# Row maxima from the high parts of q and k, with two 64-row matmuls in place of two 128-row ones

## What is computed

```
q, k, v = split_heads(x @ Wq.T), split_heads(x @ Wk.T), split_heads(x @ Wv.T)     # B=4, H=16, N=1024, d=64
s = (q @ k.T) / 8
m = max(s, axis=-1)
p = exp(s - m)
out = (p / (sum(p, axis=-1) + 1e-10)) @ v          # then @ Wo.T + bo, residual, feed-forward
```

## Time and profile before

| | |
|---|---|
| median of three runs | 1754.97 us |
| the profiled execution: its time | 1758.2 us |
| its span | 1756.4 us |
| PE (matmul) busy | 1617.6 us, 92% |
| DVE busy | 1431.2 us, 81% |
| POOL busy | 1252.1 us, 71% |
| ACT busy | 1070.3 us, 61% |
| mean granted TensorE clock | 0.977 |

### The profile page before, as it was taken

The page is one execution under the profiler, slowest core; times in us unless marked ns, Lnnn a source line. Parts: engine busy times, 40 slices in busy tenths (PEclk is TensorE's granted clock), DMA queues, the critical chain, the costliest instruction groups (busy, mean ns, idle before and its releaser), DMA issues.

```text
span 1756.4 us, 35369 instructions
## 1 busy us (share of the span) xinstructions
PE 1617.6 (92%) x13825; PEld 1192.2 (68%) x13825; DVE 1431.2 (81%) x2463; ACT 1070.3 (61%) x2222; POOL 1252.1 (71%) x1369
## 2 busy tenths in 40 slices
PE   4899999999999999999999999999999999999966
PEld 2576677777776667776667776667767676777754
DVE  7777776666788888888888888988888888888777
ACT  3466566666666656666666666665666665666533
POOL 3577777777777777777777777777777777777853
PEclk8899999999999999999999999999999999999987
DMA  5110001111111001111001111000111100111000
GB/s 133 25 25 14 19 20 26 26 25 26 26 26 27 15 15 27 27 26 27 15 16 26 27 27 25 21 20 15 27 27 26 27 15 15 27 27 26 3 4 12
DMA packets 26373, 43.24 MB, mean 25 GB/s; under 512 B 3744, under 2 KB 18016, under 8 KB 26208
## 3 DMA queue, kind: packets, MB, share of 16 engines
q1 hardware_dynamic: 26208, 40.99, 10.6%
HBM read 4.80 MB, written 2.10 MB: 4 GB/s over the span
## 4 chain that ended last, share of the span: by engine, by line
PE 52%; DVE 41%; ACT 3%; issue 2%; POOL 1%; DMA 0%; DVEq 0%; ACTq 0%; POOLq 0%
PE ob L534 14%; DVE negm L767 12%; PE sm L488 10%; PE st L506 7%; PE st L508 7%; PE mb L433 4%; DVE k_l L718 3%; DVE q_hl L718 2%; DVE xn L934 2%; PE mb L449 2%; DVE qv L919 2%; DVE q_small L915 2%; DVE qw L926 2%; PE mb L444 2%; DVE qw L924 2%
## 5 line engine op out<-in xcount | busy, mean ns | idle before, releaser
L381 POOL TENSOR_TENSOR p_low<-probs 128x512 f16<-128x512 f32 x1024 | 1086.0, 1070 | 424.5 <-ACT probs L616 422.6
L616 ACT ACTIVATE probs<-st 128x512 f32<-128x512 f32 x1024 | 607.9, 597 | 423.9 <-PE st L508 421.6
L767 DVE TENSOR_REDUCE negm<-sm 128x1 f32<-128x1024 f32 x512 | 624.6, 1220 | 150.8 <-PE sm L488 147.5
L506 PE MATMUL st<-q_hl,k_hh 128*128 128x512 f32 x1024 | 465.7, 455 | 0.0
L488 PE MATMUL sm<-k_hh,q_hl 128*128 128x512 f32 x1024 | 370.4, 443 | 65.1 <-DVE negm L767 62.4
L508 PE MATMUL st<-q_hm,k_l 66*128 66x512 f32 x1024 | 409.5, 400 | 0.0
L534 PEld LDWEIGHTS ob<-v,probs 128*128 128x128 bf16 x4096 | 236.5, 98 | 141.7 <-issue 141.7
L534 PEld LDWEIGHTS ob<-v,p_low 128*128 128x128 f16 x4096 | 234.8, 97 | 144.0 <-issue 130.2
L534 PE MATMUL ob<-v,probs 128*128 128x129 f16 x4096 | 325.1, 222 | 0.0
L534 PE MATMUL ob<-v,p_low 128*128 128x129 f16 x4096 | 323.0, 221 | 1.8 <-POOL p_low L381 1.8
L506 PEld LDWEIGHTS st<-q_hl,k_hh 128*128 128x128 f32 x1024 | 194.8, 190 | 40.6 <-issue 0.9
(11 more groups left out here) (145 smaller groups left out, 1611.2 us busy)
## 6 DMA issues: line engine op xcount, KB each, us to landing
k_hh<-k_hh SPq DMA_DIRECT2D x64, 256.0 KB, 3.3
q_hm<-q_hl SPq DMA_DIRECT2D x64, 256.0 KB, 3.4
x<-x SPq DMA_DIRECT2D x4, 512.0 KB, 7.2
q_hm<-m_high SPq DMA_DIRECT2D x128, 2.0 KB
q_hm<-m_low SPq DMA_DIRECT2D x128, 2.0 KB
out<-x SPq DMA_DIRECT2D x24, 64.0 KB, 1.5
probs<-wq SPq DMA_DIRECT2D x1, 512.0 KB, 5.6
probs<-wk SPq DMA_DIRECT2D x1, 512.0 KB, 6.8
```

Source lines behind the costliest of these rows:

```text
L381: return pool.tensor_tensor(p_low[b][:, j, :], p, p.bitcast(BF16)[:, 1::2], ALU.subtract)
L506: pe.matmul(st[s % 2][:, :], k_hh[n][:, s * P:(s + 1) * P], q_hl[n][:, half * HALF:(half + 1) * HALF], start=True, stop=False)
L616: nc.scalar.activation(probs[k % 2][:, s, :], st[s % 2][:, :], ACT.Exp, scale=SCALE).then_inc(s_ex, 1)
L767: nc.vector.tensor_reduce(negm[k % 2][:, s // 2:s // 2 + 1], sm[:, :, :].rearrange("p a n -> p (a n)"), AX.X, ALU.max, negate=True).then_i ...
```

## The change

- `scores(s)` is called in odd slots only and issues both matmuls of a pair. Each has 64 rows. The first reads `q_hl[n][0:64]` and `k_hh[n][0:64]` (q high, k high) for the first half of the keys; the second reads `q_hm[n][64:128]` and `k_hh[n][64:128]` (again q high, k high) for the second half. q low x k high is no longer in these scores. The first lies in the upper 64 rows of the array, the second in the lower 64, and they write different banks.
- `q_hm` and `k_l1` become 128 partitions high: q high and k low move to 64 to 127, the maximum and the ones to rows 0 and 1, rows 2 to 63 are zero. L508 (L514 now) is a 128-row matmul.
- The first scores of a pair of heads wait for the copy of q high (`s_dq`) and for the high parts (`s_hi`) instead of the low ones (`s_lo`).
- At the start DVE clears 64 rows of `q_hm` and of `k_l1` for each n, with a wait before the ones.

```diff
-        q_hm = [sb(f"q_hm{n}", [DH + 2, N], F32R) for n in range(4)]
+        q_hm = [sb(f"q_hm{n}", [P, N], F32R) for n in range(4)]
-        k_l1 = [sb(f"k_l1{n}", [DH + 2, N], F32R) for n in range(4)]
+        k_l1 = [sb(f"k_l1{n}", [P, N], F32R) for n in range(4)]
...
-                        sp.dma_start(q_hm[n][DH + part:DH + part + 1, half * HALF:(half + 1) * HALF].bitcast(F32)
+                        sp.dma_start(q_hm[n][part:part + 1, half * HALF:(half + 1) * HALF].bitcast(F32)
...
+                if r == 0:
+                    sp.wait_ge(s_qz, 4)
...
-                        sp.dma_start(q_hm[n + h][0:DH, :].bitcast(F32), q_hl[n + h][0:DH, :].bitcast(F32)).then_inc(s_dq, 16)
+                        sp.dma_start(q_hm[n + h][DH:P, :].bitcast(F32), q_hl[n + h][0:DH, :].bitcast(F32)).then_inc(s_dq, 16)
...
-                        if r == 0 and k == 2 and s == 0:
+                        if r == 0 and k == 2 and s == 1:
                             pe.wait_ge(s_we, 6)
-                        if k == 2 and s == 0:
-                            wait(pe, s_lo, 8 * (g + 1))
+                        if k == 2 and s == 1:
+                            wait(pe, s_hi, 8 * (g + 1))
                             wait(pe, s_dk, 32 * (g + 1))
-                        if s % 2 == 0:
-
-                            wait(pe, s_mx, 4 * (unit + 2) + s // 2)
+                            wait(pe, s_dq, 32 * (g + 1))
+
+                        wait(pe, s_mx, 4 * (unit + 2) + s // 2)
                         t = half * IT + s // 2
-                        pe.matmul(sm[:, s % 2, :], q_hl[n][:, t * P:(t + 1) * P],
-                                  k_hh[n][:, (s % 2) * 512:(s % 2 + 1) * 512], start=True, stop=True
-                                  ).then_inc(s_sm, 1)
+                        for h, q_rows in enumerate((q_hl[n], q_hm[n])):
+                            rows = slice(h * DH, (h + 1) * DH)
+                            last = pe.matmul(sm[:, h, :], q_rows[rows, t * P:(t + 1) * P],
+                                             k_hh[n][rows, h * 512:(h + 1) * 512], start=True, stop=True)
+                        last.then_inc(s_sm, 2)
...
                             if slot == 0:
-                                wait(pe, s_dq, 32 * g)
+                                wait(pe, s_lo, 8 * g)
...
-                        if has_max and not s % 2:
-                            scores(s)
...
-                nc.vector.memset(k_l1[n][DH:DH + 2, :].bitcast(F32), 1.0).then_inc(s_init, 1)
+                nc.vector.memset(q_hm[n][0:DH, :].bitcast(F32), 0.0).then_inc(s_qz, 1)
+                nc.vector.memset(k_l1[n][0:DH, :].bitcast(F32), 0.0).then_inc(s_kz, 1)
+                wait(dve, s_kz, n + 1)
+                nc.vector.memset(k_l1[n][0:2, :].bitcast(F32), 1.0).then_inc(s_init, 1)
...
-                        lo = q_hl[n][DH:P, cols] if name[0] == "q" else k_l1[n][0:DH, cols]
+                        lo = q_hl[n][DH:P, cols] if name[0] == "q" else k_l1[n][DH:P, cols]
```

More of the change, by code:

```diff
@@ L196, in build @@
         s_init = sem("ones_made")
+        s_qz = sem("max_rows_zeroed")
+        s_kz = sem("ones_rows_zeroed")
         s_dl = sem("ln_step")
```

## The result

The changed kernel takes 1779.62 us (median of 4 runs, 1778.66 to 1780.56) against 1755.34 us before: a ratio of 1.0135, 95% interval 1.0122 to 1.0148. It is 24 us slower, where 19 us less were forecast. It lies in the range that was given, but on the side of rival 4, near the price of its mild end, though not for the reason given there.

The account below looks back on a forecast made before the run. TensorE bounds, with DVE second in feed-forward rounds. 1758.2 us less 26.4 (220 pairs by 0.12) plus 7.4 for the start is 1739.2; less 3.2 to the median, about 1736; range 1700 to 1800 us (8 in 10).

Parts of the forecast that it names:

- rival 4: Row-max pair: the array is emptied at each change between 128-row and 64-row use; up to 1892 us, chance 0.26.
- its mild end: Row-max pair: only one side of it pauses, 0.14 us a pair, +25 us, 1780 us; part of rival 4.
- The sum that gave 1736 us: Whole kernel: 1758.2 - 26.4 for pairs + 7.4 for the start = 1739.2, less 3.2 to the median of runs.
- L462 passed without a pause: 32-column strip between 128-column matmuls: 0.34 us in all against 0.29 without it, taken as evidence against rival 4.
- The bound and the loop of pair and reduction: Row maxima: TensorE matmuls and DVE reduction alternate on one `sm`; DVE is the second bound, in 24 feed-forward rounds.
- The count of pairs that pass something on: DVE waits for row-max matmuls before 220 reductions, 6 in a feed-forward round; each passes its pair's saving on.
- The saving of side by side: Row-max pair: matmuls overlap but weight loads start 0.11 us apart, so 0.23 - 0.11 = 0.12 us is saved.
- rival 2: Row-max pair: weight loads side by side too, 0.28 us instead of 0.51; 1712 us, at the far end 1687; chance 0.26.
- all 54 us that TensorE waits for reductions: 77 waits of TensorE for the row-max reduction, 54.3 us in all, subtracted in full from the cost of pauses.
- Nothing: The 128-row L508 (now L514) and, in later rounds, the wait for the copy of q high: no cost.
- the copy: Copy of q high in round 0: lands 2.9 us later than q low, taken as 1.5 us, ends 0 and 2.9.
- The start: Added memsets (5.9 us) and round 0's wait for the copy of q high (1.5): about 7.4 us, bounds 5.8 and 9.

## Why the prediction was wrong

- **The step that failed** is the cost of the passage between full and 64-row use. The sum that gave 1736 us has no term for it: it went in at nothing, and stood only in rival 4, at a chance of 0.26, because L462 passed without a pause. The runs show 0.145 us on the way in and 0.195 on the way out, 0.34 in all, so that a pair costs 0.11 us more instead of 0.12 less. What I had let stand as evidence was one form of instruction, a transposing matmul; as a plain one the same strip pauses. The Trainium skill, "TensorEngine Tiling (Array Packing)", Key Properties, says that a change of tiling mode drains TensorE; the trace agrees for rows, for columns and for a plain 32-column strip.
- **The bound and the loop of pair and reduction** were read rightly. With the pair 0.11 us dearer, rounds that TensorE bounds grew by 1.38 us and feed-forward rounds by 0.48. The count of pairs that pass something on (12 and 6 a round) would give 1.3 and 0.7.
- **The saving of side by side** was taken as 0.12, because loads stood 0.11 apart in the earlier trace rows. It is 0.23: loads into different rows start together. Here rival 2 was right, and the Trainium skill, "TensorE: Matmul & The Clock Gate", Part 3, by which the second tile starts about 4 ns behind the first, agrees with the trace (3 ns in the median of 512 pairs).
- **The rivals were set against each other** though they can hold together. Full overlap and pauses at both sides give 0.34 - 0.23 = +0.11 us a pair. None of my cases was that sum. Rival 4 priced both pauses at 0.48 us with half an overlap, and came to 1892. Its mild end, 1780 us, rested on one pause and half an overlap, and met the result by luck. Its 0.14 us a pair is not even what its terms give: 0.16 + 0.05 - 0.12 is 0.09, and with that and the same waits taken off, 512 pairs come to 1754 us, no loss. It also took off all 54 us that TensorE waits for reductions, and of these only 9 went: 45.2 us are left in the middle of the changed kernel's span.
- **Nothing** for the 128-row L514 was right (397 ns against 400), and for the copy in later rounds too: with 128-row scores the rounds are the old ones. In round 0 the pair did wait for the copy, at 39.82 us, with 40 forecast, and for 2.5 us, between the 1.5 that the sum took and its upper end of 2.9.
- **The start**: 7.4 us were forecast, and the run with 128-row scores is 7.4 us slower than the kernel before, with 5 to 10 in the interval. The first statistics start at 10.80 us, as forecast. How much of this lasts to the end is less sure: with the clearing on POOL no gain clear of noise was left.

## What to carry to other kernels

Two half-height matmuls side by side do run in the time of one, but changing TensorE from full to divided use and back costs about 0.34 us in this kernel, more than one 512-column matmul. Here one pair between two passages saved 0.23 us for 0.34. By these numbers two pairs in a row would be the first to pay (0.46 us for 0.34, an estimate; no run here has more than one), so divide the array only where several matmuls run divided before it is whole again. A free passage of one form of instruction says nothing of another form.

Where TensorE is near its bound, look at what a faster piece makes it wait for, since a wait of 1.9 us in place of 0.95 was followed by the half clock. That wait came from two operations of DVE and POOL that changed places by 0.05 us: a gain on one engine can be lost by the order in which two others meet.

## What was not expected of the hardware

- The transposing form of a matmul with 4 stationary columns passes without a pause (L506 ends 0.24 us behind it), the plain form with the same shape does not (0.43 us).
- A matmul of 66 rows between 128-row ones shows no pause (0.237 us behind the one before), one of 64 rows does (0.43 us).
- Of a DVE and a POOL operation that read SBUF side by side, the one that started second paid: DVE 1.37 us instead of 0.52, or POOL 1.42 instead of 1.04, with 0.006 to 0.05 us between their starts.
- Weight loads of fp32r into the upper and the lower 64 rows start at the same time, where full ones follow 0.11 us apart.
- A bf16 reading with stride 2 of fp32r operands keeps TensorE's rate on both sides (0.23 us for 512 columns) and takes the exposed load away: 0.68 against 0.75 us.
- A memset of 1024 columns takes 0.91 us for 2 partitions and for 64, and one that waits for the memset before it starts 0.27 us behind instead of 0.16.
